# Differential attention on one Trainium2 core: the difference of two softmaxes, formed by TensorE through a diagonal matrix in place of VectorE

## The reference, cut to what matters

```python
q1, q2 = jnp.split(q12, 2, axis=-1)
k1, k2 = jnp.split(k12, 2, axis=-1)
attn1 = jnp.einsum('bqd,bkd->bqk', q1, k1) * scale
attn2 = jnp.einsum('bqd,bkd->bqk', q2, k2) * scale
lam_full = lam1 - lam2 + LAMBDA_INIT
diff = jax.nn.softmax(attn1, axis=-1) - lam_full * jax.nn.softmax(attn2, axis=-1)
out = jnp.einsum('bqk,bkd->bqd', diff, v)
rms = jnp.sqrt(jnp.mean(out * out, axis=-1, keepdims=True) + EPS)
return out / rms * (1.0 - LAMBDA_INIT)
```

## Time and profile before

| | us |
|---|---|
| median of 3 runs | 962.96 |
| the profiled execution | 964.08 |
| its span, first to last instruction | 962.2 |
| TensorE busy (mean granted clock 0.949) | 819.5 |
| VectorE busy | 701.3 |
| ScalarE busy | 552.9 |
| GpSimd busy | 528.3 |

### The profile page before, as it was taken

One profiled execution on the slowest core, in us unless ns is written; L12 is line 12 of the kernel. 1 busy time (PEld: TensorE's weight loads), 2 busy tenths in 40 slices (PEclk: granted clock), 3 DMA queues, 4 the chain that ended last, 5 costly groups with the idle time before them and its releaser, 6 DMA issues.

```text
span 962.2 us, 18279 instructions
## 1 busy us (share of the span) xinstructions
PE 819.5 (85%) x6646; PEld 537.9 (56%) x6646; DVE 701.3 (73%) x1481; ACT 552.9 (57%) x1027; POOL 528.3 (55%) x577
## 2 busy tenths in 40 slices
PE   7779997999899999999996786677898778999990
PEld 4356664448644444444543654444565547999980
DVE  5889994003798999999993769998477755657475
ACT  6566665430388788887875553444777653433420
POOL 2500005907088888888532489993047761656572
PEclk9899999999999999999999797899899997999995
DMA  6012210236122221121210995000101111332287
GB/s 162 1 45 88 89 44 23 66 131 175 46 36 36 36 36 35 36 34 27 37 24 20 164 249 174 1 1 0 45 29 54 38 50 62 97 108 89 91 245 213
DMA packets 109897, 70.62 MB, mean 73 GB/s; under 512 B 41538, under 2 KB 103436, under 8 KB 108272
## 3 DMA queue, kind: packets, MB, share of 16 engines
q1 hardware_dynamic: 99440, 60.11, 24.9%
q0 software_dynamic: 4608, 6.64, 2.1%
q10 hardware_dynamic: 5760, 2.70, 1.1%
HBM read 32.04 MB, written 31.60 MB: 66 GB/s over the span
## 4 chain that ended last, share of the span: by engine, by line
PE 50%; DVE 27%; issue 6%; POOL 4%; ACT 3%; DMA 3%; SPq 1%; ACTq 1%; POOLq 0%; DVEq 0%
PE banks L2173 7%; PE banks L2165 6%; PE banks L1975 5%; DVE B_mneg L1103 4%; PE banks L1944 3%; PE banks L1962 3%; PE banks L1921 3%; PE banks L1894 3%; PE banks L1888 2%; DVE D_dmx L1219 2%; DVE C_nmax L1041 2%; PE banks L1866 2%; PE banks L1949 2%; PE banks L2045 2%; PE banks L2096 2%
## 5 line engine op out<-in xcount | busy, mean ns | idle before, releaser
L1103 DVE TENSOR_REDUCE B_mneg<-banks 128x2 f32<-128x768 f32 (+1 forms) x128 | 136.4, 1086 | 8.0 <-PE banks L1949 4.3
L1637 ACT ACTIVATE B_pt<-banks 128x768 f32<-128x768 f32 (+1 forms) x128 | 117.2, 917 | 31.4 <-PE banks L1962 29.4
L785 POOL TENSOR_SCALAR_AFFINE_SELECT B_pt<-B_pt 128x512 f32<-128x512 f32 x128 | 80.7, 639 | 82.6 <-ACT B_pt L1637 62.8
L1975 PE MATMUL banks<-B_pt,B_vp 128*32 128x512 f32 (+3 forms) x1024 | 95.6, 444 | 0.6 <-POOL B_pt L785 0.2
L902 POOL DMA_INDIRECT rows_dram<-F_xs,F_rowi x64 | 62.5, 977 | 60.3 <-issue 59.7
L1768 ACT ACTIVATE F_gh<-banks 128x512 f32<-128x512 f32 (+1 forms) x96 | 49.4, 527 | 79.2 <-PE banks L2165 74.9
L928 POOL DMA_INDIRECT y_dram<-F_yo,F_ide x60 | 62.3, 1038 | 58.4 <-DVE F_yo L1463 41.2
L2096 PE MATMUL banks<-D_qk 128*128 128x512 f32 x128 | 74.1, 664 | 11.8 <-DVE D_pr L1230 11.8
L2173 PE MATMUL banks<-F_gw,F_gh 128*128 128x128 f32 x640 | 75.2, 275 | 0.0
L2173 PEld LDWEIGHTS banks<-F_gw,F_gh 128*128 128x128 f32 x640 | 73.9, 192 | 0.6
L1944 PE MATMUL banks<-B_kt,B_qt 64*128 64x256 bf16 (+3 forms) x512 | 72.7, 301 | 1.7 <-ACT B_pt L1637 1.2
(11 more groups left out here) (300 smaller groups left out, 2164.6 us busy)
## 6 DMA issues: line engine op xcount, KB each, us to landing
comb_dram<-C_comb SPq DMA_DIRECT2D x6, 1024.0 KB, 3.9
rows_dram<-D_zeros SPq DMA_DIRECT2D x8, 650.0 KB, 15.8
F_xe<-rows_dram SPq DMA_DIRECT2D x8, 650.0 KB, 3.9
C_w<-w_in SPq DMA_DIRECT2D x16, 256.0 KB, 3.1
C_cst<-comb_dram SPq DMA_DIRECT2D x4, 1024.0 KB, 7.7
y_dram<-D_zeros SPq DMA_DIRECT2D x2, 2048.0 KB, 17.7
F_gw<-mw_in SPq DMA_DIRECT2D x16, 256.0 KB, 3.1
F_xs<-y_dram SPq DMA_DIRECT2D x16, 256.0 KB, 4.9
```

What stands on the lines that cost most here:

```text
L785: g.affine_select(out=w, in_=w, compare_op=ALU.is_ge, fill=0.0, base=0, pattern=[[0, G], [1, P]], channel_multiplier=-1).then_inc(B_md, 1)
L1103: v.tensor_reduce(mneg[:, g % 2, :, pairs[0], qt_], scores[:, :, 0:w], X, ALU.max, negate=True).then_inc(B_mx, 1)
L1637: a.activation(pt[:, 2 * hp:2 * hp + 2, PT_AT[kt]:PT_AT[kt] + w], scores[:, :, 0:w], ACT.Exp).then_inc(B_ex, 1)
L1975: ins = t_.matmul(bank[7][SL * r:SL * r + SL, kt * P:T], vp[:, g // NG % 2, g % NG, kt, SL * r:SL * r + SL], pt[:, r, PT_AT[kt]:PT_AT[kt] ...
```

## The change

The odd exponentials go to a tile of their own in SBUF, `pr2`. VectorE no longer forms the difference: per tile it makes a 128x128 diagonal matrix `dmat` in one scalar_tensor_tensor, the identity scaled by -lam (`lam_i`, made once) times s1 times 1/s2. TensorE accumulates, per block of 128 keys, the transpose of `pr` and the product of `pr2`, as the stationary operand, with `dmat`, which is the turned and weighted second part. A score now waits for the exponential three units back, whichever unit held the bank. `difference` waits, from the second batch on, until TensorE has turned the same tile of the batch before. The plan's order of items is as it was.

```diff
--- before.py
+++ after.py
@@ -524,8 +524,10 @@
         vt = D1("vt", [P, 2, NT, D])
         pr_ = D1("pr", [P, NT, T])
         dmx, dsum = D1("dmx", [P, 8]), D1("dsum", [P, 8])
-        dinv, dco = D1("dinv", [P, 2, NT, 2]), D1("dco", [P, 2])
+        dinv = D1("dinv", [P, 2, NT, 2])
         dfT = D1("dfT", [P, 2, T])
+        pr2 = D1("pr2", [P, NT, T])
+        lam_i, dmat = D1("lam_i", [P, P]), D1("dmat", [P, NT, P])
         D_ln = sem("D_ln1_and_its_projection_in")
         D_in, D_var, D_sd, D_lam, D_le = sem("D_in"), sem("D_var"), sem("D_sd"), sem("D_lam_sums"), sem("D_lam_exp")
         D_ly, D_wq, D_z = sem("D_ly_ready"), sem("D_wq_scaled"), sem("D_rows_cleared")
@@ -1223,12 +1225,13 @@
                 dve.wait_ge(D_ex, D_PLAN.nth("s", "s", b, u + 1))
                 if b == 0 and t == 0:
                     dve.wait_ge(D_le, 3)
+                    own.link(v.tensor_scalar(lam_i[:], ident[:], lms[:, 5:6], None, ALU.mult))
                 own.link(v.reciprocal(dinv[:, b % 2, t, :], dsum[:, u:u + 2]))
-                own.link(v.tensor_scalar(dco[:, t % 2:t % 2 + 1], dsum[:, u:u + 1], dinv[:, b % 2, t, 1:2], lms[:, 5:6],
-                                         ALU.mult, ALU.mult))
-                second = bank[2 + (D_PLAN.nth("s", "s", b, u + 1) - 1) % 3][:]
-                v.scalar_tensor_tensor(out=pr_[:, t, :], in0=second, scalar=dco[:, t % 2:t % 2 + 1],
-                                       in1=pr_[:, t, :], op0=ALU.mult, op1=ALU.add).then_inc(D_df, 1)
+                if b:
+                    dve.wait_ge(D_tf, D_PLAN.nth("T", "T", b - 1, t))
+                v.scalar_tensor_tensor(out=dmat[:, t, :], in0=lam_i[:], scalar=dsum[:, u:u + 1],
+                                       in1=dinv[:, b % 2, t, 1:2].broadcast_to([P, P]), op0=ALU.mult, op1=ALU.mult
+                                       ).then_inc(D_df, 1)
 
             def outputs(b):
                 dve.wait_ge(D_wf, D_PLAN.nth("w", "w", b, NT - 1))
@@ -1688,7 +1691,7 @@
                     act.wait_ge(D_tf, D_PLAN.nth("T", "T", b - 1, u // 2))
                 act.wait_ge(D_mx, n)
                 scores = bank[2 + (n - 1) % 3][:]
-                a.activation(pr_[:, u // 2, :] if u % 2 == 0 else scores, scores, ACT.Exp, bias=dmx[:, u:u + 1],
+                a.activation((pr_, pr2)[u % 2][:, u // 2, :], scores, ACT.Exp, bias=dmx[:, u:u + 1],
                              accum_out=dsum[:, u:u + 1]).then_inc(D_ex, 1)
 
             def difference_T(b, t):
@@ -2086,10 +2089,7 @@
             def scores(b, u):
                 t, h = divmod(u, 2)
                 n = D_PLAN.nth("s", "s", b, u)
-                old = D_PLAN.back("s", ("s", b, u), 3)
-                if old and old[2] % 2:
-                    pe.wait_ge(D_df, D_PLAN.nth("c", "c", old[1], old[2] // 2))
-                elif old:
+                if n > 3:
                     pe.wait_ge(D_ex, n - 3)
                 if u < 2:
                     pe.wait_ge(D_ma, D_PLAN.nth("act", "P", b, 2 + u))
@@ -2102,7 +2102,9 @@
                 if n > 1:
                     pe.wait_ge(D_te, n - 1)
                 for m in range(NT):
-                    ins = t_.transpose(bank[1][:, m * P:(m + 1) * P], pr_[:, t, m * P:(m + 1) * P], ident[:])
+                    dst, keys = bank[1][:, m * P:(m + 1) * P], slice(m * P, (m + 1) * P)
+                    t_.matmul(dst, pr_[:, t, keys], ident[:], is_transpose=True, start=True, stop=False)
+                    ins = t_.matmul(dst, pr2[:, t, keys], dmat[:, t, :], start=False, stop=True)
                 ins.then_inc(D_tf, 1)
 
             def weigh(b, t):
```

## The result

In the runs of one chip the changed kernel took 977.07 us in the median (968.1 to 978.42, 4 runs) and the kernel before 963.33 (962.06 to 964.07): **slower by 1.4% in the medians**, and by 1.0% in the ratio (1.0101, interval 1.0065 to 1.0137). The forecast was 958.9, the range 954 to 967. The profiled execution took 976.76, its span is 975.0, 12.8 over that of before. Medians in this text are over all executions of a kernel, while the ratios leave out those over 1.5% above the kernel's shortest and aren't exactly the quotient of the medians.

A forecast was written before the change was run, and what follows sets the result against it. Two chains meet near 791 us, and only an earlier first scatter was taken to help. Its terms, -2.2 - 0.7 - 1.5 + 0.2 + 0.9 - 0.7, gave -4.0: 962.96 to 958.9 us, range 954 to 967.

The forecast's parts named there:

- the price of VectorE's new operations: Attention differences on VectorE: each new one takes 0.43 us, 0.73 saved; scaled identity about 0.3 us once, costing nothing.
- Chain A: Path from GpSimd's products and VectorE's reductions through router and 64 scatters to the expert rows; first scatter 4.0 us earlier.
- (a, b, c): VectorE's savings before the router: -2.2 us before the group maximum, -0.7 before a batch's outputs, -1.5 before the last group's.
- (a): GpSimd's shift after VectorE's group maximum: three shorter differences bring it 2.2 us earlier, at most 2.98.
- c +0.2: TensorE from 653.8 to 671.5: three turns add 2.7 us against 2.5 of idle, so 0.2 later.
- d +0.9: TensorE's gapless stretch until the root before the router: one turn in it makes it 0.9 us later.
- I let it fall again, 0: TensorE's clock after its 4.5 us wait for a batch's outputs: falls as before, 0 gained; 1.4 us if not.
- rival 2: No change: six turns from 641 to 675, 5.3 us, eat the 5.1 saved; 963 us, chance 0.18.
- The turn: TensorE's turning of each difference: four added matmuls take 0.89 us, so 0.44 becomes 1.33.
- rival 4: TensorE's added part costs double, 0.83 us more per turn; 973.7 us, chance 0.04.
- Chain B: TensorE's remaining attention beside the scatters: 79.0 us of work, ending 0.5 later, inside the 1.56 in hand.
- rival 1: TensorE bounds the last stretch: 13.4 us of added turns come on top; 970.8 us, chance 0.17.

The follow-up runs named there:

- e2_matrix_on_act: The changed kernel, but VectorE makes only a 128x1 coefficient and ScalarE the diagonal matrix: 964.8 us, ratio 1.0006 against the kernel before.
- e3_accum: The changed kernel with ScalarE making the scaled identity and VectorE each matrix by a tensor-scalar with accumulator output: 962.58 us, ratio 0.9986 against the kernel before.
- e1_lam_on_act: The changed kernel with the scaled identity made by ScalarE, the 32 matrices still on VectorE: 974.76 us, ratio 1.0125 against the kernel before.
- h4_first_four: The kernel before with the first four of eight batches combined by TensorE with ScalarE's matrix, the others keeping the old difference: 963.27 us, ratio 1.0002.
- e5_before_plus_pe: The kernel before with four fp32 matmuls by a zero matrix added to each TensorE turn, VectorE unchanged: 969.33 us, ratio 1.0065.
- the last five batches: The kernel before with only the last five of eight batches combined by TensorE with ScalarE's matrix: 971.28 us, ratio 1.0068.
- e6_after_no_matmuls: The changed kernel without TensorE's second matmuls, VectorE still making scaled identity and matrices: 974.68 us, ratio 1.0038 against the kernel before.
- e7_act_no_matmuls: e2_matrix_on_act without TensorE's second matmuls, so ScalarE makes the matrix and TensorE only transposes: 956.06 us.
- p1: The kernel before with one unused 128x128 scalar_tensor_tensor added to each of 32 differences, both inputs in SBUF: 989.83 us.
- p2: The kernel before with one unused 128x128 scalar_tensor_tensor added to each of 32 differences, first input in PSUM: 975.13 us.

## Why the prediction was wrong

- **The step that failed: the price of VectorE's new operations.** "The 128-wide operation isn't in the trace", bounded by 0.23 and 0.75 and taken at 0.30 less the 0.07 by which a successor starts early, and "the scaled identity is made once, about 0.3 us near 570 us, while GpSimd, which sets the pace there, has its queue full: nothing". Alone the operation takes 0.35, so the duration was right. But beside GpSimd's products it took up to 6.2 and the identity 10.8. The full queue that was to cover it is what it waited for. Both bounds came from operations with nothing of the sort at stake: one has an input in PSUM and the other stood where GpSimd had no products. The identity lasted 10.5 us and the matrices up to 672 together 9 us over their own work: 19.5, against the 16.5 between the forecast of -4.0 and the +12.5 measured at the first scatter. None of the four rivals had this wait, and the range ended 10 us short.
- **Chain A, the saving (a, b, c).** Right in kind where the wait is gone, and if anything too small. In e2_matrix_on_act GpSimd runs without a gap until its last group, its shift comes at 649.07, 2.9 earlier and within 0.1 of the bound that (a) gave, where the forecast had 2.2, and the last products stand 5.1 earlier.
- **Chain A, TensorE's part (c +0.2, d +0.9, "two turns ... in a wait: nothing").** Right in some traces, wrong in others. After the change the way from the last products to the first scatter is 48.1 us, for 48.3 before. In e3_accum, which has every added turn and no wait, the first scatter stands at 703.95, 3.9 earlier for the 4.0 forecast, and that execution took 960.84 for the 960.1 forecast; but it was the shortest of ten. What the sum had no term for is how long the clock stays down: "I let it fall again, 0" took it that its fall would cost what it had cost before, and in e1_lam_on_act, e2_matrix_on_act and h4_first_four it cost some 4 us more (and 2 to 3 more in kernels without added turns there). By the medians the outcome without the failed step would have been 962.6 to 964.8 (e3_accum and e2_matrix_on_act), "no change" and not 958.9. That is the time of rival 2, but not its mechanism: in e2_matrix_on_act nothing was eaten on the way to the last products.
- **The turn.** Right: TensorE's timeline after the change goes from 590.09 to 591.95 in one turn with the clock falling in it, and at full clock a transpose and its two records take 0.33; a whole turn at full clock, in the kernel with four batches, goes from 675.32 to 676.64, 1.32 us for the 1.33 forecast. Neither the double price (rival 4) nor the bare weight loads came. In the timeline (start, duration):

```profile
590.26 0.39 PE L2107 MATMUL banks<-D_dmat,D_pr 128*128 128x128 f32 x2
590.48 0.27 PE L2106 MATMUL banks<-ident,D_pr 128*128 128x128 f32 x1
590.59 0.39 PE L2107 MATMUL banks<-D_dmat,D_pr 128*128 128x128 f32 x2
```

- **Chain B and the last stretch.** Right for the changed kernel. 79.0 us of TensorE work were forecast, 79.17 measured, at a clock of 1.00. The 64 scatters stay gapless, the waits of scores for the difference are gone, and VectorE waits longer for the expert rows, so rival 1 is out there (2.64 for the 1.56 of the earlier trace rows). It isn't out in general: in e2_matrix_on_act, in e5_before_plus_pe and with the last five batches VectorE waited for its own work and not for the rows, and the expert stage began 2.1 to 4.3 us later than before. After the change:

```profile
808.62 0.81 DVE L1448 TENSOR_SCALAR F_xeT<-banks,D_lnc 128x512 f32<-128x512 f32 x1 [2.64 <-PE banks L2153]
```

## What to carry to other kernels

Before a VectorE operation is priced, look at where its inputs lie and what GpSimd does at that moment: an operation that had one input in PSUM and now has two in SBUF can wait for GpSimd's whole run, and the time of before cannot show it. If it must stand there, use one of the forms that didn't wait here (an operand in PSUM, a tensor-scalar with an accumulator output) or give it to ScalarE; one SBUF input alone is no safeguard, as the plain tensor-scalar of the scaled identity waited too. Where a change moves work from one engine to another, try it only in the stretch where the relieved engine sets the pace: here 12 of 32 differences give 5 to 8 us, and all 32 give nothing. And before a few us between two traces are put down to an edit, compare TensorE's granted clock in the same stretch of both, and of kernels that don't have the edit.

## What the runs showed that was not expected

- A VectorE operation of 0.35 us that began beside a run of GpSimd products lasted, in five cases, until the whole run ended: 2.93, 4.01, 6.25, 10.37 and 10.81 us. Others of the same line lasted 0.9 or 1.2. The difference between runs of one kernel is large where this happens: 961.0 to 982.9 in ten executions of e6_after_no_matmuls, against 954.7 to 958.1 in e7_act_no_matmuls.
- The wait came with two wide SBUF inputs (p1) and with a plain tensor-scalar of one SBUF input (the scaled identity, 10.8), and did not come with a PSUM input (p2) or with the accumulator form (e3), 0.35 in all 32 each.
- After waits of TensorE of some 3 and 1 us the granted clock stood at 0.50 for 6.9 us in one kernel and for 13.6 in another, in the second with TensorE busy without a gap for the last 11 of them. Seventeen traces fall into two groups by it, and which one a trace falls into didn't follow from the work added before it.
